# A two-layer attention and mixture-of-experts program on one core: normalisation, splitting and gate work of the first attention move from VectorE to GpSimd and ScalarE, statistics are taken in small steps, pieces are laid out by batches in DRAM, and the planner gets other durations

## The reference, cut to what matters

```python
h = _layernorm(x, axis=-1) * (1 + ca) + sa
x = x + ga * _L0_attn_ref(h, ...)
h = _layernorm(x, axis=-1) * (1 + cb) + sb
x = x + gb * _L0_ffn_ref(h, ...)
# layer 1 has the same form with _L1_attn_ref and _L1_ffn_ref
```

```python
logits = jnp.einsum('bqhd,bkhd->bhqk', Q, K) * scale          # 16 heads of 8 features
attn = jax.nn.softmax(jnp.where(causal, logits, -jnp.inf), axis=-1)
h = x @ dp_w1 + dp_b1                                          # 64 features
h = (h - mu) / jnp.sqrt(var + LN_EPS) * ln_g + ln_b
drift = (_gelu(h) @ dp_w2 + dp_b2)[..., 0]
g = _gelu(drift[..., None] * g_w1[0] + g_b1)
gate = jnp.tanh(g @ g_w2 + g_b2)[..., 0]                       # one number for each token
out = einsum(attn * gate, V) @ Wo + bo
```

## Time and profile before

| | us |
|---|---|
| three runs | 1141.25, 1143.27, 1143.30 |
| median | 1143.27 |
| the profiled execution | 1145.11 |
| its span, first to last instruction | 1143.2 |

### The profile page before, as it was taken

The page is one execution under the profiler, slowest core; times in us unless marked ns, Lnnn a source line. Parts: engine busy times, 40 slices in busy tenths (PEclk is TensorE's granted clock), DMA queues, the critical chain, the costliest instruction groups (busy, mean ns, idle before and its releaser), DMA issues.

```text
span 1143.2 us, 20670 instructions
## 1 busy us (share of the span) xinstructions
PE 953.2 (83%) x7903; PEld 780.6 (68%) x7903; DVE 726.7 (64%) x2478; ACT 550.8 (48%) x899; POOL 276.5 (24%) x351
## 2 busy tenths in 40 slices
PE   3677878878889999999999999999999924399970
PEld 2334545545567998888988898989889812299970
DVE  7879898886638547576756666766758675222225
ACT  2346657675674564554455544555455511244420
POOL 8202111020010001020403122130403140286550
PEclk9668998988999999999999999999999965599995
DMA  6532321354382000000000000000000020112217
GB/s 165 164 120 86 113 91 53 112 161 130 99 211 74 1 1 1 1 1 1 20 1 20 1 15 6 5 16 2 19 1 20 1 91 0 48 43 85 71 47 228
DMA packets 93819, 66.47 MB, mean 58 GB/s; under 512 B 7346, under 2 KB 87333, under 8 KB 93722
## 3 DMA queue, kind: packets, MB, share of 16 engines
q1 hardware_dynamic: 89236, 56.85, 17.1%
q0 software_dynamic: 4352, 8.28, 2.2%
q10 hardware_dynamic: 134, 0.04, 0.0%
HBM read 33.82 MB, written 31.59 MB: 57 GB/s over the span
## 4 chain that ended last, share of the span: by engine, by line
PE 59%; DVE 20%; ACT 6%; SPq 4%; issue 3%; DMA 2%; POOL 1%; POOLq 0%; DVEq 0%; ACTq 0%
PE psum L1335 21%; PE psum L1312 17%; DVE maxes L1653 4%; PE psum L1105 2%; PE psum L1167 2%; PE psum L1075 1%; PE psum L1387 1%; PE psum L1226 1%; SPq L975 1%; ACT ew L2085 1%; PE psum L1246 1%; PE psum L1268 1%; DVE tmp L1491 1%; DVE ew L1617 1%; DMA q_stack<-m_pieces 1%
## 5 line engine op out<-in xcount | busy, mean ns | idle before, releaser
L1335 PEld LDWEIGHTS psum<-ew,big 128*128 128x128 f32 x2560 | 320.4, 191 | 23.2 <-DVE hT L1776 5.4
L1335 PE MATMUL psum<-ew,big 128*128 128x128 f32 x2560 | 326.4, 275 | 3.7 <-DVE hT L1776 3.7
L2183 ACT ACTIVATE big<-psum,cols 128x512 f32<-128x512 f32 x256 | 175.4, 690 | 189.2 <-PE psum L1312 188.4
L1312 PE MATMUL psum<-parts,q_stack 128*128 128x512 f32 x640 | 226.9, 436 | 0.6 <-DVE parts L1977 0.5
L1312 PE MATMUL psum<-parts,k_stack 128*128 128x512 f32 x320 | 126.6, 396 | 0.0
L1653 DVE TENSOR_REDUCE maxes<-psum 128x4 f32<-128x1024 f32 (+1 forms) x96 | 113.5, 1215 | 11.2 <-PE psum L1121 11.0
L1312 PEld LDWEIGHTS psum<-parts,q_stack 128*128 128x128 f32 x640 | 103.3, 192 | 11.8 <-ACT big L2183 1.8
L2433 POOL DMA_INDIRECT routed<-big,slot_i x64 | 63.0, 985 | 96.3 <-DVE big L1971 79.2
L1776 DVE SCALAR_TENSOR_TENSOR hT<-psum,gates,hT 128x128 f32<-128x128 f32 x256 | 71.8, 343 | 22.7 <-PE psum L1335 22.7
L2085 ACT ACTIVATE ew<-psum 128x1024 f32<-128x1024 f32 x56 | 56.4, 1027 | 40.8 <-PE psum L1148 40.6
L2443 POOL DMA_INDIRECT answers<-hT,to x64 | 62.2, 972 | 36.2 <-issue 16.9
(11 more groups left out here) (351 smaller groups left out, 1733.3 us busy)
## 6 DMA issues: line engine op xcount, KB each, us to landing
q_stack<-q_pieces SPq DMA_DIRECT2D x32, 192.0 KB
k_stack<-k_pieces SPq DMA_DIRECT2D x32, 192.0 KB
routed<-empty_row SPq DMA_DIRECT2D x4, 1040.0 KB, 11.8
big<-routed SPq DMA_DIRECT2D x16, 260.0 KB, 2.8
answers<-gb_tok SPq DMA_DIRECT2D x4, 1024.0 KB, 9.9
q_pieces<-gb_tok SPq DMA_DIRECT2D x8, 384.0 KB, 3.6
k_pieces<-gb_tok SPq DMA_DIRECT2D x8, 384.0 KB, 3.5
x<-in_L_attn_x SPq DMA_DIRECT2D x4, 512.0 KB, 6.1
```

The source lines that it names most:

```text
L1312: last = eng.matmul(bank(i), w1_part(wp, e)[:, fs], parts[2 * xk + xp][:, :], start=n == 0, stop=n == 2)
L1335: last = eng.matmul(psum[:, i, k * C:(k + 1) * C], hid[:, r, f, k * P:(k + 1) * P], ew2[:, e, f, :], start=f == 0, stop=f == FC - 1)
L2183: eng.activation(hid[:, held("hid", "up", n, e, f), f, :], bank(held("bank", "up", n, e, f)), ACT.Relu, bias=col("L0_ffn_b1", e * FC + f)) ...
```

## The change

1. `ln_z` of the first normalisation becomes `ln_p` on POOL. The statistics ahead of it are split: `moment` (mean and variance of one batch) and `stat` (the root), now for 4, 4, 8, 8 and 8 tiles (`FIRST`) in place of eight times 4.
2. Of the chunks, only the first is cut by DVE; for the others POOL takes off the first piece too (`rest`), ahead of `cut`.
3. `gv_n` is dropped; `gv_a` on POOL gets two more instructions over a whole 128x512 tile. The statistics of the gate are split in the same way (`gv_m`, `gv_s`).
4. The first bf16 piece of the maxima is made by ACT instead of DVE.
5. The pieces are laid out in DRAM with the batch ahead: a `write` for each batch (6 DMAs for a chunk and matrix, 256 elements in a run, before 3 with 512), and a `stack` reads 2048 elements in a run for a row, before eight runs of 256.
6. The modulation's inputs are loaded and turned ahead of the other columns (`conds`); the masks are built behind `ln_p` 1; DVE does the four stores of -1 at the start.
7. Nearly all planned durations change, `HOP` goes from .15 to .2, the first attention's ranks and leads change (`LEAD` 5 to 6). So the order on every engine changes through the whole program, though not what is computed behind the first attention.

```diff
-CUT_BY_DVE = 2
+CUT_BY_DVE = 1
+FIRST = ((0, 4), (4, 8), (8, 16), (16, 24), (24, 32))
-    HOP = 0.15
+    HOP = 0.2
-    p.step("consts", work="pool:23")
+    p.step("pads", work="pool:5.5")
+    p.step("masks", work="pool:9.5", after=[("ln_p", 1)])
...
-                p.step("proj", n, w, work="pe:.86 act:1.35 dve:.75", urgent=3, after=needs, rank=-4,
+                p.step("proj", n, w, work="pe:.9 act:1.15", urgent=3, after=needs, rank=60 * (BPC * n - 3) + 4,
+                p.step("rest", n, w, work="pool:1.2", urgent=3, after=[("proj", n, w)], tmp=tile)
+                p.step("cut", n, w, work="act:.53 pool:1.15", urgent=3, after=[("rest", n, w)], closes=[(1, tile)], tmp=tile)
...
-            p.step("max", b, u, work="pe:.5 dve:1.25", after=...)
+            p.step("max", b, u, work=f"pe:{.52 if u < 2 else .42} dve:1.14", urgent=2, after=...)
...
-                        eng.dma_start(dst[r][at, :, :], src[n, :, j, :, :, ts]).then_inc(
+                        eng.dma_start(dst[r][at, :, :], src[n, b % BPC, :, j, :, :, :]).then_inc(
...
+            for r in range(QR):
+                last = eng.memset(k_heads[r][:, :, :], -1.0)     # on DVE, ahead of all else
+            last.then_inc(minus, 1)
...
-                eng.tensor_copy(m_pieces[:, b % 2, 0, :], m).then_inc(chain.sem, chain.more())
-                w.wait_ge(chain.sem, chain.n)
                 eng.tensor_tensor(m_pieces[:, b % 2, 1, :], m, m_pieces[:, b % 2, 0, :], ALU.subtract).then_inc(sem("mrow"), 1)
...
+            def ln_p(b):                                          # on POOL
+                k = held("tmp", "ln_p", b)
+                w.wait_ge(*done("stat", 0, 0, first_group(b)))
+                for n in range(TPB):
+                    t = TPB * b + n
+                    last = eng.tensor_scalar(T(k)[:, n * C:(n + 1) * C], x[:, t, :], mv[:, t, 0:1], rstd[:, t:t + 1],
+                                             ALU.subtract, ALU.mult)
+                last.then_inc(sem("ln_p"), 1)
+            def rest(n, wh):
+                t = T(held("tmp", "rest", n, wh))[:, :]
+                w.wait_ge(*done("proj", n, wh, by="act"))
+                eng.tensor_tensor(t, t, pieces[wh][0], ALU.subtract).then_inc(sem("rest"), 1)
             def gv_a(n):
+                eng.tensor_tensor(t3, vd[:, ts, C:VW], dmv[:, ts, 0:1].to_broadcast([P, GT, HID]),
+                                  ALU.subtract).then_inc(chain.sem, chain.more())
+                eng.tensor_tensor(t3, t3, drs[:, ts].unsqueeze(2).to_broadcast([P, GT, HID]),
+                                  ALU.mult).then_inc(chain.sem, chain.more())
```

450 lines of the change are left out of this document (239 added, 211 removed).

## The result

The change made the kernel slower by a little: 1147.64 us (median of 20 runs, 1145.65 to 1151.38) against 1143.21 for the kernel before in runs beside them, a ratio of 1.0036 with a 95% interval of 1.0023 to 1.0049. Forecast were 1116.5 us and a gain. The profiled execution after took 1149.69 us, with a span of 1147.9.

The account below looks back on a forecast made before the run. No engine was a hard bound in the steady batches; DVE was fullest and PE waited for its maxima. Preparation -13, batches -18.8, rest 0 and fills +5 sum to -26.8 us, median 1143.27 to 1116.5, range 1098 to 1140.

Parts of the forecast that it names:

- The start: Preparation ahead of the first attention: four edits bring the first `exp` to 57 us, about 13 us sooner, bounds 5 and 20.
- (a): Preparation: the modulation's inputs come first, shortening ACT's 6.55 us wait; gain taken as 4 us, between 0 and 6.5.
- (b): Preparation: stores of -1 move from POOL to DVE ahead of the first statistics; cost taken as nothing, at most 7.5 us.
- (c): Preparation: first stack issued at about 31.5 us as before, first `max` 5.5 us later (bounds 4 and 9.5), at 37.
- (d): Preparation: third chunk leaves PE's queue among the first `max` steps; first to third takes 2.4 us, not 11.1, gaining 8.7.
- The eleven batches: Steady batches of the first attention: relieving DVE shortens each from 16.4 to 14.7 us, 18.8 us less in all.
- POOL beside DVE: Steady batches: POOL holds up some small DVE instructions, priced at 0.6 us a batch, hidden by DVE's 3.7 us of room.
- The rival that had POOL hold the batch: Steady batches: DVE's small instructions meet POOL's runs each time and lengthen the batch; +9 us, 1152 us; chance 7%.
- The last four batches: End of the first attention: left at 57.6 us, no change, because DVE already had room there.
- The fills: Behind the first attention: PE's stall grows from 3.3 to about 8 us, 5 us lost, bounds 0 and 12.
- The rest: Behind about 340 us: PE is full and its work unchanged, so zero, bounds -4 and 4 us.
- the second rival: Steady batches: PE's queue order, bank pairs and the maxima's transfer already set 16.4 us; -8 us, 1135 us; chance 20%.

Follow-up runs that it names:

- e5: Changed kernel planned with the old durations from the output projection on, and the third expert-weight load moved behind the maxima of batch 13; 1148.55 us, ratio .9634.
- e4: Changed kernel with each fill planned at 14 us of transfer instead of 9, so `sg_m` comes later; 1162.73 us, ratio .9789.
- b1: Kernel before, order kept, with seven of eight `gv_n` tiles and 480 of 512 columns of the cut's first subtraction left out; ratio .9961.
- g2: Changed kernel planned with `HOP` 0.15 instead of 0.2; ratio .9958, eleven batches 190.7 us.
- p1: Changed kernel, order kept, with nearly all of `rest` and two of `gv_a`'s four instructions left out on POOL; ratio .9890.
- e1: Changed kernel with the third expert-weight load moved behind the maxima of batch 13 in SP's order; ratio .9898.
- f1: Kernel before with the smaller DVE work of b1 and the gate's two `Gelu` computed as `Tanh`; ratio .9886, eleven batches 168.5 us.
- g3_before: Kernel before, unchanged, profiled once on a chip other than the first; its eleven batches take 181.4 us.

## Why the prediction was wrong, by its own steps

**The start: right in its sum, not in its parts.** -11.9 us against -13, the first `exp` at 58.29 against 57. (a) The modulation gained 2.3 us, not 4: ACT still stood 5.20 us. (b) The stores of -1 were priced at nothing, and they are what (a) waited for. DVE's timeline after:

```profile
1.29 1.76 DVE L1522 MEMSET k_stack<- 128x2048 bf16 x1 [1.29 <-PEq L2538]
...
9.40 0.42 DVE L1576 BATCH_NORM_STATS2 stats<-x 128x6 f32<-128x128 f32 x2
```

and POOL's, with the first `ln_p`:

```profile
13.33 3.35 POOL L2378 TENSOR_SCALAR ew<-x,mv,rstd 128x128 f32<-128x128 f32 x4 [9.11 <-DVE rstd L1538]
```

Four stores of 1.76 us, 2.14 us apart, kept DVE until 9.40 us, where the first statistics stood at 5.35 before; `ln_p` waited for the statistics, PE for `ln_p`, and ACT for PE. From 1.29 us on that is 8.1 us, more than the upper bound of 7.5. The Trainium skill's table (VectorE: DVE Perf Modes, perf-mode tier table) has 693 ns for a bf16 copy of that size, and the prediction's estimate of 2.8 us for four stores was made from it. The trace shows no such copy, and for these stores the estimate does not hold. (c) The stack was issued at 31.74 as forecast (31.5), but the first `max` came at 41.17, not 37. The profile names nothing that PE stood for in the 3.68 us ahead of it, so whether the runs of 2048 elements landed sooner is not shown. What did get shorter is the issue: the eight reads of the first stacks took SP 6.1 us (31.74 to 37.80) and before 10.7 (31.62 to 42.30). (d) The third `max` came 1.7 us behind the first and not 11.1: 9.4 us gained, 8.7 forecast. From there to the first `exp` it took 15.5 us, not 18.0. Then 4.9 us that no term had went between the first `exp` and the first `oc`: 3.39 us of idle PE against 0.48, with 1.86 for the pieces at 70.81, and 2 us more of PE's work.

**The eleven batches: the step that failed first.** 10 us of the forecast gain are missing, by two steps of the sum. "Of its idle time I take away what it waited for DVE" took 17.8 us; 13.3 went. And PE's busy time was left at the 12.87 us a batch of the kernel before, less a little for the clock, where it rose by 4.4 us. The prediction says that one chunk less is projected at the start and calls that "part of the 14.7", but no term of the sum has it: the six `ln_t`, `val` and `proj` groups in place of five are 4.2 us at the durations before. (At the same clock of .92 PE is busy for 144.2 and 144.4 us in e5 and e4 and for 141.2 to 141.9 in the order of before; the chunk covers that too.)

The first step is wrong in its reason and not only in its size. b1 took 16 us from DVE and PE's idle time did not fall; in g2, with the changed kernel's instructions in another order, it is 34.8 us. So DVE's load alone was not what PE stood for. How much of the 13.3 us came by the new order, and how much by the order and the lighter engines together, is not separated, and how an order makes PE wait less is open. The sign that the prediction itself had named, a batch of 16 us with DVE at 70%, came: 15.6 us at 74%. "That is the sign of what is left when DVE has room", said of the 14.4 us in the last four, was the false inference behind it: those batches have other work in PE's list, with no projection in it. The sizes on the other engines were right or near: POOL 6.2 against 5.5 a batch (`ln_p` took 0.79 us an instruction, where 0.48 was taken), ACT 10.95 against 10.9, DVE 11.6 against 10.96, the last two with one chunk's work more than in the window of before.

**POOL beside DVE: right, and without weight.** One meeting, DVE's timeline after:

```profile
103.27 0.17 DVE L1649 TENSOR_SCALAR dmv<-dmv 128x8 f32<-128x8 f32 x1
103.48 1.13 DVE L1527 TENSOR_SCALAR dln_tmp<-dmv 128x8 int32<-128x8 int32 x1
104.64 1.14 DVE L1530 TENSOR_SCALAR drs<-dln_tmp 128x8 int32<-128x8 int32 x1
105.82 0.17 DVE L1534 SCALAR_TENSOR_TENSOR dln_tmp<-drs 128x8 f32<-128x8 f32 x1
```

and POOL's:

```profile
103.43 1.15 POOL L2390 TENSOR_TENSOR gb_tok<-ew,gb_tok 128x512 bf16<-128x512 f32 x1 [1.41 <-ACT gb_tok L2101]
104.60 1.16 POOL L2385 TENSOR_TENSOR ew<-ew,gb_tok 128x512 f32<-128x512 f32 x1
```

A DVE instruction of 128x8, of which the others take 0.17 us, takes as long as the one of POOL beside it, twice in a row. This is what the Trainium skill (SBUF: State Buffer, its section on two separate sides) says of the shared ports, an exclusive lock for a whole instruction, and the trace agrees. The groups of maxima stay at 1.217 us each, against 1.214. DVE's room hid it: with 17 us less on POOL (p1) the batches take 171.9 us and not 171.7. The rival that had POOL hold the batch did not come.

**The last four batches: forecast 0, measured +11.7.** This is the largest miss. "The last four batches I leave at 57.6 us; DVE had room there" is the step: it asked only whether DVE had room, and did not look at what the new order put on SP ahead of the pieces. PE's idle time rose by 6.8 us (7.6 to 14.4). The wait at 268.71 is 5.3 us longer than the longest wait for pieces before, and the waits for maxima rose from 1.8 to 5.3 us; others fell. PE's busy time rose by 4.9 us, at a clock of .88 against .94, with some 2 us of steps that the kernel before did behind this stage. Of the wait, e1's edit took 3.3 us away.

**The fills: right in mechanism and size.** ACT waited 8.90 us (forecast 9), PE stood 8.78 (forecast 8) and lost 3.5 on balance (forecast 5, bounds 0 and 12). e4 takes the stall away again.

**The rest: +5.3, just outside its bounds of 4.** The last `up` gives 2.2 of them (its step on ACT stands at 912.4 against 910.8), the chain of the last chunk 2.8 and the second mixture 2.0, less 1.7 in the output. No run takes these parts on the first chip one by one, so their cause is open.

Of the cases named, the second rival ("the batches don't get shorter", 1135 us) came nearest to the mechanism of the batches (the order of PE's queue, with DVE's work in its gaps), though they did get 0.8 us shorter each, and it had nothing for the last four. None had a stage grow by the order alone.

## What to carry to other kernels

An engine with the largest busy share, named in the largest waits, need not set the pace: leave its work out once (b1 did so with two edits) before moving it, and then together with the next engine's, as in f1. Where a planner writes the order, compare a change of arithmetic with a change of order alone on the same chip, for the second can be the larger. When a change takes work out of one stage, count the same instructions in the next one. And for every small transfer on the path, read what stands ahead of it on its queue in the new order.

## What was not expected of the hardware

- The issue of a small DMA directly behind one of about 1 MB took 9.57 us on SP; two of them ahead of it took 1.19, and before, 2.5 us behind it, two took 2.77.
- A store of 128x2048 in bf16 took 1.76 us on DVE (2.14 from one to the next) and 1.87 on POOL.
- The kernel before took 1143 us on one chip and 1182 to 1190 on five others with the same first attention. In g3_before 17 us of it lie between 345 us and the last `up` and 16 in the second mixture; its cause is open.
